# Self-attention projections in three products of parts, and expert stages of 79 and 23 blocks

## What is computed

```python
# layer 0
x = x + self_attention(ln(x), Wq, Wk, Wv, Wo)   # 16 heads of 32, causal, q and k rotated (rope)
x = x + cross_attention(ln(x), ctx)             # 16 heads of 32, int8 fake-quantized projections
x = x + experts(ln(x))                          # 8 experts, top 2, y = silu(a) * b @ w2, width 352
# layer 1
x = x + self_attention(ln(x), w_project, w_out) # same shape, no rope
x = x + cross_attention(ln(x), ctx)             # 16 heads of 128, RMS norm of q and k, image and text
x = x + experts(ln(x))                          # 32 experts, top 6, relu, plus 2 shared experts
```

## Time and profile before

| | |
|---|---|
| runs | 3081.09, 3088.36, 3082.03 us; median 3082.03 |
| profiled execution | 3078.52 us, its span 3076.7 us |
| instructions | 47541 |
| mean granted clock of TensorE | 0.943 of full |

### The profile page before, as it was taken

The page is one execution under the profiler, slowest core; times in us unless marked ns, Lnnn a source line. Parts: engine busy times, 40 slices in busy tenths (PEclk is TensorE's granted clock), DMA queues, the critical chain, the costliest instruction groups (busy, mean ns, idle before and its releaser), DMA issues. The chain is left out here.

```text
span 3076.7 us, 47541 instructions
## 1 busy us (share of the span) xinstructions
PE 2767.7 (90%) x15658; PEld 1978.0 (64%) x15658; DVE 1461.4 (47%) x2628; ACT 1288.5 (42%) x2906; POOL 1108.3 (36%) x1023
## 2 busy tenths in 40 slices
PE   7987999996699598879999989999998879999997
PEld 3453443432588345568877879999997647777762
DVE  3475436775211307678874337776663441111115
ACT  2462524554111126556652228888882202222220
POOL 2352225664111205435553445555551011212116
PEclk9899999997699798999999999999999889999998
DMA  2342424310599413156666773444431119999986
GB/s 92 70 96 82 161 87 102 64 32 4 183 326 317 155 41 83 43 181 237 236 235 192 222 233 139 184 186 174 170 150 59 50 54 339 345 346 346 345 272 210
DMA packets 320543, 526.50 MB, mean 171 GB/s; under 512 B 35778, under 2 KB 169282, under 8 KB 312228
## 3 DMA queue, kind: packets, MB, share of 16 engines
q1 hardware_dynamic: 292004, 453.61, 45.2%
q0 software_dynamic: 13440, 44.05, 4.7%
q10 hardware_dynamic: 14976, 27.27, 2.4%
HBM read 369.52 MB, written 130.02 MB: 162 GB/s over the span
## 5 line engine op out<-in xcount | busy, mean ns | idle before, releaser
L1741 PE MATMUL ps<-moe_blocks_xgt,moe_blocks_w 128*128 128x128 f32 (+1 forms) x3072 | 362.8, 277 | 7.1 <-DMA moe_blocks_b1s<-rb_cols 4.3
L1741 PEld LDWEIGHTS ps<-moe_blocks_xgt,moe_blocks_w 128*128 128x128 f32 (+1 forms) x3072 | 350.4, 184 | 10.3 <-issue 10.1
L2670 POOL TENSOR_TENSOR normed<-normed,xa_core_rinv 128x257 f32<-128x257 f32 (+1 forms) x256 | 260.6, 1041 | 214.0 <-DVE xa_core_rinv L2594 214.0
L1812 DVE COPY moe_blocks_y<-ps 128x512 f32<-128x512 f32 x104 | 72.0, 692 | 454.3 <-PE ps L1723 454.3
L1723 PE MATMUL ps<-moe_blocks_w,moe_blocks_ht 128*128 128x512 f32 (+1 forms) x624 | 285.0, 593 | 0.0
L550 POOL TENSOR_TENSOR sa_w<-sa_w,sa_core_rinv 128x256 f32<-128x256 f32 (+3 forms) x128 | 159.4, 1254 | 236.5 <-DVE sa_core_rinv L497 236.5
L1689 POOL COPY moe_blocks_idx<-moe_index 128x1 uint32 (+1 forms) x104 | 19.2, 185 | 561.8 <-PE ps L1714 435.2
L2650 ACT ACTIVATE normed<-normed,xa_core_nmax,xa_rq 128x257 f32<-128x257 f32 (+1 forms) x256 | 206.8, 810 | 4.2
L2282 POOL TENSOR_TENSOR normed<-normed 128x512 f32<-128x512 f32 x96 | 150.5, 1568 | 116.9 <-DVE normed L2235 116.9
L1762 ACT ACTIVATE moe_blocks_xgt<-ps 128x512 f32<-128x512 f32 x104 | 62.1, 597 | 304.1 <-PE ps L1714 304.1
L787 DVE TENSOR_REDUCE xa_nmax<-ps 128x1 f32<-128x1024 f32 x128 | 149.2, 1217 | 58.6 <-PE ps L778 58.6
(11 more groups left out here) (333 smaller groups left out, 6525.3 us busy)
## 6 DMA issues: line engine op xcount, KB each, us to landing
moe_blocks_w<-L_ffn_rw SPq DMA_DIRECT2D x80, 704.0 KB
moe_blocks_w<-L_ffn_rw SPq DMA_DIRECT2D x80, 512.0 KB
moe_blocks_w<-L_ffn_w SPq DMA_DIRECT2D x24, 1408.0 KB
k_parts<-xa_parts SPq DMA_DIRECT2D x64, 512.0 KB, 3.3
v_parts<-xa_v_parts SPq DMA_DIRECT2D x128, 256.0 KB, 2.7
xa_parts<-k_parts SPq DMA_DIRECT2D x32, 1024.0 KB
xa_core_v<-v_parts SPq DMA_DIRECT2D x32, 1024.0 KB
moe_y<-moe_blocks_y ACTq DMA_DIRECT2D x104, 256.0 KB
```

The costliest lines, as they stand in the source:

```text
L1741: mm = nc.tensor.matmul(g.ps[0:fn, 2 + s % 2 + 2 * half, f * P:(f + 1) * P], w1s[s][:, k, half * F + f0:half * F + f0 + fn], xgt[:, s % 2, ...
L2670: ins = nc.gpsimd.tensor_tensor(prob[:, n % PR, lo:hi], prob[:, n % PR, lo:hi], rinv[:, n % PR, m:m + 1].to_broadcast([P, hi - lo]), ALU.mult)
```

## The change

Three edits. (1) The transposed rows and the weights of both self-attention projections are split into high and low parts, and each f32 product becomes three fp32r products. The rows' high part is written by ScalarE's eviction in the layer norm, their low part by VectorE from PSUM; the weights' parts are made in the projection stage, one block of 128 columns (128 x 512 elements) at a time, into buffers that hold one of q, k, v at a time. The block for unit pair p+4 is split as soon as the second unit of pair p is made. The rope buffers move into `g.xt`, which is free now. (2) The second pack's buffer is allocated in the core stage only, so the pack of head group 1 moves from the end of the projection stage to the start of the core stage. (3) `blocks_bound` isn't rounded up any more: 79 and 23 blocks, and the last ring has three slots. The router's tables keep an even number of columns, 80 and 24.

```diff
+            def low(dve, t):
+                dve.wait_ge(high_done, t + 1)
+                cols = slice(t * P, (t + 1) * P)
+                nc.vector.tensor_tensor(parts[1][:, :, cols], g.ps[:, t % 4, :].rearrange("p (k c) -> p k c", k=KC),
+                                        parts[0][:, :, cols], ALU.subtract).then_inc(copied, 1)
+
             @block.vector
             def _(dve):
                 for t in range(NT):
                     nc.vector.tensor_scalar(xn[:, t, :], g.x[:, t, :], g.mv[:, t, 0:1], g.rstd[:, t:t + 1],
                                             ALU.subtract, ALU.mult).then_inc(normed, 1)
+                    if parts is not None and t >= 2:
+                        low(dve, t - 2)
+                for t in range(NT - 2, NT if parts is not None else 0):
+                    low(dve, t)
 
             @block.scalar
             def _(act):
                 for t in range(NT if turn else 0):
                     act.wait_ge(turned, t + 1)
-                    nc.scalar.activation(g.xt[:, :, t * P:(t + 1) * P],
+                    out = g.xt if parts is None else parts[0]
+                    nc.scalar.activation(out[:, :, t * P:(t + 1) * P],
                                          g.ps[:, t % 4, :].rearrange("p (k c) -> p k c", k=KC),
-                                         ACT.Copy).then_inc(copied, 1)
+                                         ACT.Copy).then_inc(copied if parts is None else high_done, 1)
 
             @block.tensor
...
-        layer_norm(nc, g, name + "_ln", prefetch=load_weights)
         with Stage(nc, name + "_proj") as pr:
-            project_self(nc, g, pr, w, w_loaded, rope, qk, v, wos, wo, wo_loaded, masks, mask, heads)
+            x_high, x_low = pr.sbuf("x_high", [P, KC, T], F32R), pr.sbuf("x_low", [P, KC, T], F32R)
+            layer_norm(nc, g, name + "_ln", prefetch=load_weights, parts=(x_high, x_low))
+            project_self(nc, g, pr, x_high, x_low, w, w_loaded, rope, qk, v, wos, wo, wo_loaded, masks, mask, heads)
         with Stage(nc, name + "_core") as co:
             self_core(nc, g, co, heads, v, ot, masks, w)
...
         self.parts = [st.sbuf(f"parts{n}", [P, 4, S], F32R) for n in range(2)]
-        self.packed = [st.sbuf(f"packed{n}", [self.ROWS, HPC, 2, S], F32R) for n in range(2)]
+        self.packed = []
+        self.grow(st)
         self.high_done, self.low_done = st.sem("high_done"), st.sem("low_done")
         self.packed_in = [st.sem(f"packed_in{n}") for n in range(2)]
+
+    def grow(self, st):
+        n = len(self.packed)
+        self.packed.append(st.sbuf(f"packed{n}", [self.ROWS, HPC, 2, S], F32R))
 
     def high(self, nc, i):
...
     if rope:
         cos, sin, swap = st.sbuf("cos", [P, S]), st.sbuf("sin", [P, S]), st.sbuf("swap", [P, P])
-        raw, rc, rs = st.sbuf("raw", [P, RAW, S]), st.sbuf("rc", [P, 2, S]), st.sbuf("rs", [P, 2, S])
+        free = g.xt[:, :, :].rearrange("p k (a n) -> p (k a) n", n=S)
+        raw, rc, rs = free[:, 0:RAW, :], free[:, RAW:RAW + 2, :], free[:, RAW + 2:RAW + 4, :]
         swapped, cos_done, sin_done, rotated = (st.sem("swapped"), st.sem("cos_done"), st.sem("sin_done"),
                                                 st.sem("rotated"))
     r_loaded = st.sem("r_loaded")
+    w_high, w_low = st.sbuf("w_high", [P, KC, D], F32R), st.sbuf("w_low", [P, KC, D], F32R)
+    w_highs, w_lows = st.sem("w_highs"), st.sem("w_lows")
+
+    def high_columns(act, q):
+        part, c = divmod(q, KC)
+        if c == 0:
+            act.wait_ge(w_loaded[part], 16)
+        nc.scalar.activation(w_high[:, :, c * P:(c + 1) * P], w[:, :, q * P:(q + 1) * P], ACT.Copy).then_inc(w_highs, 1)
+
+    def low_columns(dve, q):
+        c = q % KC
+        dve.wait_ge(w_highs, q + 1)
+        nc.vector.tensor_tensor(w_low[:, :, c * P:(c + 1) * P], w[:, :, q * P:(q + 1) * P],
+                                w_high[:, :, c * P:(c + 1) * P], ALU.subtract).then_inc(w_lows, 1)
+
     with nc.Block() as block:
         @block.sync
...
             heads.pack(sp, 0)
-            heads.pack(sp, 1)
             sp.wait_ge(wo_loaded, 32)
...
                                  stop=True).then_inc(swapped, 1)
 
             for j, (c, b, dst, part) in enumerate(units):
-                if j % 8 == 0:
-                    pe.wait_ge(w_loaded[part], 16)
+                if b == 0:
+                    pe.wait_ge(w_lows, j // B + 1)
                 if j >= 4:
                     pe.wait_ge(copied, j - 3)
+                cols, rows = slice(c * P, (c + 1) * P), slice(b * S, (b + 1) * S)
                 for k in range(KC):
-                    mm = nc.tensor.matmul(g.ps[:, j % 4, :], w[:, k, part * D + c * P:part * D + (c + 1) * P],
-                                          g.xt[:, k, b * S:(b + 1) * S], start=(k == 0), stop=(k == KC - 1))
+                    mm = split_matmul(nc, g.ps[:, j % 4, :], w_high[:, k, cols], w_low[:, k, cols], x_high[:, k, rows],
+                                      x_low[:, k, rows], start=(k == 0), stop=(k == KC - 1))
                 mm.then_inc(made, 1)
                 if rope and j >= 1:
                     swap_pairs(j - 1)
             if rope:
                 swap_pairs(len(units) - 1)
-            pe.wait_ge(w_loaded[2], 16)
+            pe.wait_ge(w_lows, 3 * KC)
             for t in range(NT):
                 if t >= 2:
                     pe.wait_ge(v_copied, t - 1)
+                rows = slice(t * P, (t + 1) * P)
                 for k in range(KC):
-                    mm = nc.tensor.matmul(g.ps[:, 6 + t % 2, :], g.xt[:, k, t * P:(t + 1) * P], w[:, k, 2 * D:3 * D],
-                                          start=(k == 0), stop=(k == KC - 1))
+                    mm = split_matmul(nc, g.ps[:, 6 + t % 2, :], x_high[:, k, rows], x_low[:, k, rows], w_high[:, k, :],
+                                      w_low[:, k, :], start=(k == 0), stop=(k == KC - 1))
                 mm.then_inc(v_made, 1)
 
         @block.scalar
         def _(act):
+            for q in range(KC):
+                high_columns(act, q)
             for j, (c, b, dst, part) in enumerate(units):
                 act.wait_ge(made, j + 1)
...
+                if b == B - 1:
+                    high_columns(act, KC + j // B)
             for t in range(NT):
...
+            for q in range(KC):
+                low_columns(dve, q)
+            for j, (c, b, dst, part) in enumerate(units):
+                if b == B - 1:
+                    low_columns(dve, KC + j // B)
+                if rope:
+                    if j == 0:
+                        dve.wait_ge(r_loaded, 48)
+                    dve.wait_ge(swapped, j + 1)
+                    nc.vector.tensor_tensor(rs[:, j % 2, :], g.ps[:, 4 + j % 2, :], sin[:, :],
+                                            ALU.mult).then_inc(sin_done, 1)
+                    dve.wait_ge(sin_done, j + 1)
+                    dve.wait_ge(cos_done, j + 1)
+                    nc.vector.tensor_tensor(dst[:, b * KC + c, :], rc[:, j % 2, :], rs[:, j % 2, :],
+                                            ALU.add).then_inc(rotated, 1)
             heads.low(nc, dve, 0)
             heads.low(nc, dve, 1)
...
         def _(sp):
-            for i in range(2, NI):
-                sp.wait_ge(scores, U * (i - 1))
+            for i in range(1, NI):
+                if i >= 2:
+                    sp.wait_ge(scores, U * (i - 1))
                 heads.pack(sp, i)
...
 def blocks_bound(experts, top_k):
 
-    most = (T * top_k + experts * (P - 1)) // P
-    return -(-most // 4) * 4
+    return (T * top_k + experts * (P - 1)) // P
...
     R = 4
-    NR = blocks // R
+    NR = -(-blocks // R)
+    TAIL = blocks - R * (NR - 1)
...
                 step(i, s)
-        for s in range(R):
-            step(NR - 1, s, last=(s == R - 1))
+        for s in range(TAIL):
+            step(NR - 1, s, last=(s == TAIL - 1))
 
     with nc.Block() as block:
...
             rings(act, step)
-            store(NR - 1, R - 2)
-            store(NR - 1, R - 1)
+            store(NR - 1, TAIL - 2)
+            store(NR - 1, TAIL - 1)
             for s in range(R):
-                act.wait_ge(y_stored[s], 16 * NR)
+                act.wait_ge(y_stored[s], 16 * (NR if s < TAIL else NR - 1))
 
         @block.vector
...
     blocks = blocks_bound(experts, top_k)
+    columns = blocks + blocks % 2
     y_dram = nc.dram_tensor(name + "_y", (blocks * P, D), F32, kind="Internal").ap()
     rows_dram = nc.dram_tensor(name + "_rows", (T, D), F32, kind="Internal").ap()
```

More of the change, by code:

```diff
@@ L144, in layer_norm @@
         normed, turned, copied = st.sem("normed"), st.sem("turned"), st.sem("copied")
+        high_done = st.sem("high_done") if parts is not None else None
         rows_stored = st.sem("rows_stored")
@@ L1695, in step @@
                 pool.wait_ge(idx_put, j + 1)
-                if s < R - 1:
-                    put(i, s + 1)
-                elif not last:
-                    put(i + 1, 0)
```

(5 more changed lines are left out.)

25 lines of the change are left out of this document (8 added, 17 removed).

## The result

The changed kernel took 3052.26 us (median of four runs, 3049.99 to 3058.46) against 3083.82 us before (four runs, 3081.09 to 3088.36): 31.6 us less. 3051.3 had been predicted. The two spans, 3056.3 and 3076.7 us, are therefore only 20.4 us apart, and a sum over stages explains 20, not 31.

What follows compares the result with a forecast made beforehand. TensorE was taken to bound both projection and both block stages. -34.1 -14.0 +6.3 +3.0 +4.1 +4.0 = -30.7 us on 3078.52 gives 3047.8, for a median 3051.3; range 3041 to 3066.

Steps and rivals of the forecast that it cites:

- Products of parts, -34.1: Both self-attention projections: a unit of 12 rounded products takes 2.72 us instead of 3.43, 48 units, 34.1 us less.
- Rival (d): Projections: the weight load is not hidden, a unit takes 5.00 us, 109 us over forecast, 3160; chance 0.01.
- The layer norm, +6.3: Layer norms ahead of both projections: eight added VectorE subtractions from PSUM lengthen each by 3.15 us, 6.3 together.
- First split, +3.0: Start of both projections: the first product waits 1.5 us for one column block's high and low parts, 3.0 together.
- The wait before V, +4.1: Before the V products: the last weight block splits after the last QK unit; TensorE idles 2.3 and 1.8 us.
- The clock at the starts, +4.0: Both projections' starts: idle of about 3.6 us lowers TensorE's clock, 2 us lost a stage, bounds 0 and 6.1.
- Rival (a): Projections' starts: the clock does not fall, total 3047.3 us; chance 0.25.
- a granted clock below 1 after the first 6 us of a projection: Both projections: listed as a sign in the profile after that the prediction would be wrong.
- Group 1's pack, 0: Core stage's start: the moved pack lands at 128.2, before its first reader at 133.53; margin 5.3 us, cost nothing.
- The blocks, -14.0: Expert stages: one block less in each, periods 8.34 and 5.70 us, 14.0 us less, bounds 13 and 15.
- rival (e): Expert stages: no gain, as a block less only exposes what DMA still owes; -16.7, total 3065; chance 0.03.
- Elsewhere: Low clock stretches, as in the first core stage, may fall elsewhere once everything shifts: 0, with 4 us either side.

Runs made afterwards that it cites:

- experiment 8: Changed kernel plus, per projection, six unread transposes behind the layer norm's last tile and five unread products at the projection's start; 3047.77 us, ratio 0.9887.
- experiment 12: Changed kernel plus only six unread transposes behind each layer norm's last tile, without the five products; 3055.78 us, ratio 0.9907.
- Experiment 7: Changed kernel with head group 1's pack held back until six scores of group 0 are done; 3063.38 us, ratio 0.9941.
- experiment 1: Kernel before with only the expert part of the change, 79 and 23 blocks; 3070.99 us, ratio 0.9956.
- experiment 4: Changed kernel with five column slots and the first column block's weights split inside the layer norm, normalized rows in q's buffer; 3043.03 us, ratio 0.9871.
- experiment 3: Changed kernel with a fifth column slot for the weights' parts, so V's last block is split earlier; 3044.22 us, ratio 0.9874.
- Experiment 6: Kernel before with four blocks more in each expert stage, 84 and 28; 3144.31 us, ratio 1.0201.
- experiments 2: Changed kernel with the block bound of before, 80 and 24 blocks: projections in parts and moved pack only; 3069.85 us, ratio 0.9957.
- experiment 5: Changed kernel run again without edit, on the second chip; 3058.77 us, ratio 0.9924.
- experiment 10: Changed kernel with five column slots and the first weights split inside the layer norm, run a second time, on the third chip; 3050.81 us, ratio 0.9884.
- experiment 9: Changed kernel run a third time without edit, on the third chip; 3053.16 us, ratio 0.9903.
- experiment 11: Changed kernel with five slots, early first split and six unread transposes behind each layer norm's last tile; 3044.23 us, ratio 0.9878.

## Why the prediction was right, and where its terms were off

It was right in the time (3051.3 against 3052.26) and, term by term, mostly by its own steps. That the two agree within 1 us is luck in part: the forecast was 30.7 us less, and the three comparisons gave 31.6, 30.6 and 24.6.

- **Products of parts, -34.1.** 2.73 us per unit against 2.72; rotated units 3.63 against 3.58, which is 0.8 us over 16 units. The estimate from the four passes of the Trainium skill (FP8 and Floating Point Precision, TensorE Precision Notes) was 2.57; the trace does not agree. Rival (d), the weight load in series, is excluded by the same steps of 0.227 us, with which the Trainium skill's rule on LDWEIGHTS (TensorE: Matmul & The Clock Gate, what overlaps and what doesn't) does not agree either.
- **The layer norm, +6.3**: +3.3 and +2.9, by the chain that was forecast.
- **First split, +3.0**: the stage of after begins at 24.57 and its first product at 26.07, 1.50 us later, as the chain of the earlier trace rows has it. Before, the first product came 0.12 us behind the stage's start, so the cost is 1.38 us a stage, 2.8 together.
- **The wait before V, +4.1**: 1.37 and 1.93, together 3.3. Without rope the eviction starts 0.04 us behind the last product, and rounding, subtraction and next product start 0.49, 0.65 and 0.75 us after one another: 1.93 us, where I had added 0.60, 1.5 and a hop of 0.2.
- **The clock at the starts, +4.0**: 1.35 and 2.5 us in the profile of after, 3.8. Rival (a), that it does not fall, is out; experiment 8, which fills the idle stretch and adds transposes ahead of it, shows that it can be taken away: 2.0 and 3.8 us a stage, the V stretch included. Whether the idle time or the sparse transposes ahead of it bring the clock down is not separated: with six more transposes alone (experiment 12) it stayed up at one start and fell at the other. **What I had not foreseen** is a third low stretch, behind the V wait without rope: 1.7 us. It comes 51 us into the stage and is one of the prediction's own signs of being wrong (a granted clock below 1 after the first 6 us of a projection): I had priced the wait, and put at nothing what the clock does behind it. With it the second projection is 74.99 us, where my terms make 84.0 - 17.05 + 1.5 + 2.3 + 2 = 72.75; the first, where it did not come, is 85.86 against 86.1. The closeness of these two is luck as well: in the four other profiles with these projections it takes 86.6 to 87.2.
- **Group 1's pack, 0**: no wait. Experiment 7 took the cover away and found waits of 2.1 and 3.1 us, and 4.0 and 6.7 us in the cores.
- **The blocks, -14.0**: -13.4 alone. The first stage kept its period of 8.34 us, and is 7.5 to 8.8 us shorter in the eleven profiles with 23 blocks. The second gave 1.7 in the profile of after and 4.8 in experiment 1. Neither is the price of a block: over the profiles with 79 blocks the stage takes 471.2 to 477.8 us (eleven, mean 473.8), and the two with 80 take 477.4 and 483.3. Most blocks there evict 5.6 to 5.8 us apart, as the earlier trace rows have it, and a few do not. The longest stands near the end. Timelines of TensorE's first products of that block and VectorE's evictions around it, before and then after:

```profile
2958.71 4.50 PE L1741 MATMUL ps<-moe_blocks_xgt,moe_blocks_w 128*128 128x128 f32 x24 [1.94 <-DMA moe_blocks_b1s<-rb_cols]
...
2956.45 0.69 DVE L1812 COPY moe_blocks_y<-ps 128x512 f32<-128x512 f32 x1 [4.98 <-PE ps L1723]
2965.89 0.69 DVE L1812 COPY moe_blocks_y<-ps 128x512 f32<-128x512 f32 x1 [8.75 <-PE ps L1723]
```
```profile
2941.73 2.92 PE L1788 MATMUL ps<-moe_blocks_xgt,moe_blocks_w 128*128 128x128 f32 x24 [0.24 <-DMA moe_blocks_b1s<-rb_cols]
2949.49 4.32 PE L1788 MATMUL ps<-moe_blocks_xgt,moe_blocks_w 128*128 128x128 f32 x24 [1.82 <-DMA moe_blocks_b1s<-rb_cols]
...
2947.27 0.69 DVE L1859 COPY moe_blocks_y<-ps 128x512 f32<-128x512 f32 x1 [5.40 <-PE ps L1770]
2956.68 0.69 DVE L1859 COPY moe_blocks_y<-ps 128x512 f32<-128x512 f32 x1 [8.73 <-PE ps L1770]
```

This block took 9.44 us before and 9.41 after, instead of 5.7, so it is no part of the difference between the two. TensorE waited 1.94 and 1.82 us for the block's loads (the trace names the bias as the last to land; weights and bias share SP's queue), and then the 24 records took 4.50 and 4.32 us instead of 2.8 or 2.9, with a stretch at granted clock 0.50 in them. One block between the 73rd and the 78th is such a one in all fourteen profiles. It takes 7.4 to 12.7 us, and in thirteen of them a wait of 1.8 to 4.0 us for loads stands ahead of it. The low clock follows in ten: behind a wait of 2.1 us the block takes 8.06 us without it (experiment 4) and 9.69 with it (experiment 3). What makes the loads late at this place is open.

What after has besides are two blocks of 7.39 and 7.19 us, each behind a wait of 1.3 or 1.4 us for its loads; before has none like them. They cost 3.2 of the 4.0 us that the second stage fell short. With DMA at 0.99 of its share over the stage, the stream of weights has little slack, and how many such waits there are differs between executions. My rival (e), that the stages gain nothing, is out; but the busy share with which I excluded it can't see these: a product slowed by the clock is busy. Experiment 6 puts a block there at 6.6 to 8.1 us in stage time when four are added, a time in which such stalls are part of the price.
- **Elsewhere**, 0 with 4 us to either side: the first cross-attention's projections took 159.83 us in after, 4.4 more than before. The code of this stage is the same in all kernels. Yet it takes 155.38 to 155.45 us in the three profiles with the old self-attention projections (before, experiments 1 and 6), and 155.75 to 159.86, mean 158.1, in the eleven with products of parts. One wait of TensorE some 63 us into the stage tells them apart. Timeline, before and after:

```profile
360.12 6.28 PE L1076 MATMUL ps<-xa_proj_wkv,xa_proj_ctx 128*128 128x512 f32 x14 [1.52 <-DVE xa_v L958]
```
```profile
354.15 6.20 PE L1122 MATMUL ps<-xa_proj_wkv,xa_proj_ctx 128*128 128x512 f32 x7 [3.15 <-DVE xa_v L1004]
```

It is 1.52 to 1.54 us in the three and 2.54 to 3.18 us in the eleven. A low stretch follows in eight of the eleven, after among them, where 6.2 us hold 7 records instead of the 14 before; only those eight stages take more than 156 us. So the rival of experiments 2 and 5, that the new projections lengthen this stage, holds in part: 0.3 to 4.4 us. Why VectorE's eviction comes later there is not known. These 4.4 us and the 4.0 of the second expert stage are 8.4 of the 10.3 us by which the profiled execution of after (20.4) falls short of the sum of my terms (30.7).

**What stays open** is why the change gives 24.6 us on one chip and 30.6 and 31.6 in the other comparisons (the intervals 0.9911 to 0.9937 and 0.9883 to 0.9923 overlap), and what puts a run on one or the other of two levels in experiments 3, 4 and 10. The levels go with the mean granted clock of the whole run: 0.944 and 0.943 in the two shorter runs of experiment 10 and 0.938 in the four longer ones, 0.940 to 0.946 against 0.939 and 0.937 in experiment 4, 0.941 and 0.942 against 0.938 and 0.937 in experiment 3. The five runs of experiment 5 have 0.938 to 0.940, the four of experiment 9 0.940 to 0.942, so the chip with the smallest gain also has the lower clock. In the profiles of single executions, time that differs lies in low stretches of the clock in untouched stages and in DMA waits of the last blocks. What decides how much of a run is at 1.2 GHz was not tested.

## What to carry to other kernels

Cost a split into parts by the kernel's own rows for the same call and shape, and cost its preparation as chains (eviction, rounding, subtraction, product): each of these terms came out within about a microsecond that way. Where TensorE begins a dense stretch behind a few idle microseconds, look at the starts of its first products: if they come twice as far apart, a handful of products that nobody reads can be worth more than it costs (11.0 us in experiment 8; the transposes alone brought nothing in experiment 12), and moving the preparation ahead of the barrier as well shortens the stages further. Compare the stages that the change does not touch too: one of them was 0.3 to 4.4 us longer here in every profile with the new projections. Do not take a TensorE that is busy 99% of a stage as proof that DMA sets nothing there, and before a long block is made the reason of a difference, look for it in the kernel before.

## What the runs showed of the hardware that I had not expected

- The clock falls after short idle stretches: 3.49 us, 2.11 us and, in the five profiles whose layer norm had no filler, 1.93 us were followed by products 0.43 us apart; 1.57 us before the change and 1.46 us in experiment 11 were not, nor 2.84 us behind six more transposes, at the first start of experiment 12. The same 1.93 us brought no low clock in experiments 8 and 12, whose fillers stood some 50 us earlier. In the first cross-attention 1.52 us brought none, and 2.54 to 3.18 us did in eight profiles of eleven. It is not the idle time alone, and what it is was not tested further.
- Twenty-two matmuls and transposes added to TensorE, the engine that bounds the projection stages, made the kernel 11.0 us faster (experiment 8 against 5).
- A wait of 1.82 us for a DMA stood in a block that took 3.7 us longer than its neighbours: about half is the wait, and most of the rest the lower clock of the products behind it. The kernel before has the same block, with 1.94 us and 9.44.
